# Two-layer transformer kernel on one Trainium2 core: TensorE's order of jobs, scores, weighted sums and transposes written out anew for both layers, and v read where it lies

## What is computed

```
x = x + attn_a(layernorm(x))      # scores over all 1024 keys
x = x + ffn(layernorm(x))
x = x + attn_b(layernorm(x))      # keys after the query masked
x = x + ffn(layernorm(x))

attn: qkv = x @ Wqkv + b; scores = q.k / sqrt(8); softmax; times v; @ Wout + bout
ffn:  (silu(x @ wg.T) * (x @ wu.T)) @ wd.T     # HIDDEN = 384
```

## Time and profile before

| | |
|---|---|
| median of 3 runs | 1573.65 us (1570.76 to 1574.26) |
| the profiled execution | 1573.21 us; span from first to last instruction 1571.4 us |
| TensorE (PE) busy | 92% of the span |
| VectorE (DVE) busy | 79% |
| ScalarE (ACT) busy | 62% |
| GpSimd (POOL) busy | 7% |
| granted clock of TensorE, mean | 0.965 of full |

### The profile page before, as it was taken

How to read it: one execution, slowest core, us unless ns; L and a number is a source line. 1 busy time by engine, 2 the same in 40 slices (tenths; PEclk the granted TensorE clock), 3 DMA queues, 4 the chain that set the end, 5 groups by cost and what they waited for, 6 DMA issues and landing times.

```text
span 1571.4 us, 26128 instructions
## 1 busy us (share of the span) xinstructions
PE 1438.6 (92%) x9625; PEld 701.7 (45%) x9625; DVE 1235.9 (79%) x3106; ACT 980.0 (62%) x1259; POOL 108.9 (7%) x210
## 2 busy tenths in 40 slices
PE   3699999999999999999988988999999999999888
PEld 2444344434444443444436654444444444444455
DVE  7589999999999998999937757787787877777254
ACT  4427777777777777777774432666666666666622
POOL 6020000000000000000001112000000000000010
PEclk9859999999999999999999985999999999999999
DMA  3720111111101111110001323111121112210000
GB/s 95 221 57 7 27 28 29 29 29 28 28 6 25 28 28 29 28 28 2 2 1 54 83 79 76 35 29 29 29 53 32 29 29 47 38 29 2 8 21 27
DMA packets 40055, 58.39 MB, mean 37 GB/s; under 512 B 7796, under 2 KB 19448, under 8 KB 39928
## 3 DMA queue, kind: packets, MB, share of 16 engines
q1 hardware_dynamic: 39928, 56.72, 15.2%
HBM read 36.77 MB, written 18.87 MB: 35 GB/s over the span
## 4 chain that ended last, share of the span: by engine, by line
PE 70%; DVE 18%; ACT 5%; issue 4%; DMA 2%; SPq 1%; POOL 0%; DVEq 0%; ACTq 0%; POOLq 0%
PE psum L995 25%; PE psum L1045 23%; DVE maxima L785 11%; PE psum L1009 6%; PE psum L1142 5%; PE psum L938 4%; ACT probs L559 3%; DVE junk L782 3%; PE psum L1147 2%; PE psum L1017 1%; PE psum L948 1%; DVE xn L706 1%; PE psum L1062 1%; DMA k_parts<-parts 1%; DMA qop<-shift_rows 1%
## 5 line engine op out<-in xcount | busy, mean ns | idle before, releaser
L559 ACT ACTIVATE probs<-psum 128x1024 f32<-128x1024 f32 (+3 forms) x896 | 794.2, 932 | 300.4 <-PE psum L1009 192.7
L785 DVE TENSOR_REDUCE maxima<-psum 128x1 f32<-128x512 f32 x1280 | 815.2, 684 | 72.8 <-PE psum L995 67.8
L995 PE MATMUL psum<-kop,qop 62*128 62x512 f32 (+3 forms) x1792 | 657.0, 465 | 56.5 <-DVE maxima L782 20.0
L1009 PE MATMUL psum<-qop,kop 64*128 64x512 f32 (+3 forms) x1792 | 498.2, 411 | 10.4 <-ACT probs L559 7.8
L995 PEld LDWEIGHTS psum<-kop,qop 62*128 62x128 f32 x1792 | 289.6, 191 | 487.6 <-DVE maxima L785 325.4
L1045 PE MATMUL psum<-probs,vwin 128*32 128x512 f32 (+3 forms) x3584 | 441.6, 565 | 3.9 <-ACT probs L559 2.0
L782 DVE CUSTOM_DVE_ANT_0 junk<-psum,mask 128x384 bf16<-128x384 f32 (+3 forms) x512 | 237.4, 487 | 75.3 <-PE psum L995 69.8
L1009 PEld LDWEIGHTS psum<-qop,kop 64*128 64x128 f32 x1792 | 242.0, 189 | 55.7 <-ACT probs L559 44.7
L1045 PEld LDWEIGHTS psum<-probs,vwin 128*32 128x32 f32 x3584 | 71.8, 109 | 105.5 <-issue 84.6
L1017 PE MATMUL psum<-half_ident,key_mask 64*128 64x64 bf16 x1024 | 92.7, 198 | 0.0
L1142 PE MATMUL psum<-ffn_xt,wffn 128*128 128x512 f32 x192 | 87.6, 594 | 0.0
(11 more groups left out here) (88 smaller groups left out, 709.9 us busy)
## 6 DMA issues: line engine op xcount, KB each, us to landing
qop<-q_parts SPq DMA_DIRECT2D x256, 64.0 KB
q_parts<-parts SPq DMA_DIRECT2D x32, 256.0 KB, 3.0
k_parts<-parts SPq DMA_DIRECT2D x32, 256.0 KB, 3.4
kop<-k_parts SPq DMA_DIRECT2D x64, 128.0 KB
kop<-k_parts SPq DMA_DIRECT2D x128, 64.0 KB
x<-in_L_attn_a_x SPq DMA_DIRECT2D x8, 256.0 KB, 4.4
qop<-shift_rows SPq DMA_DIRECT2D x128, 8.0 KB
out_x<-x SPq DMA_DIRECT2D x8, 256.0 KB, 2.3
```

The costliest lines, as they stand in the source:

```text
L559: nc.scalar.activation(probs[:, slot, :, c0:], psum[:, bank:bank + 2, c0:], ACT.Exp, scale=SCORE_SCALE).then_inc(probs_ready, 1)
L785: nc.vector.tensor_reduce(dst, src, AX_X, ALU.max).then_inc(ring_free, 1)
L995: mm(psum[:, slot, 0:width], qop[rows, buf, f, r, qb * P:(qb + 1) * P].bitcast(F32R), kop[rows, buf, r, kh * CHUNK:kh * CHUNK + width].bit ...
L1009: ins = mm(psum[:, bank + h, c0:], kop[rows, buf, pair, j * P:(j + 1) * P].bitcast(F32R), qop[rows, buf, f, pair, c0:].bitcast(F32R), star ...
```

## The change

The placement by weights is gone. Each layer's plan now has a string of letters for one turn: `j` a job, `s` a unit of scores, `p` the sums of a step, `H` and `h` the shift transposes (of the next window's half 0, of this window's half 1), `N` and `n` the transposes of the sums (this window's half 0, the last window's half 1). All engines walk the list that comes of it.

- Layer 0: the sums run two steps behind the scores (one before). 46 jobs stand ahead of the first scores.
- Layer 1: the sums stay one step behind. 44 jobs ahead. `alternate` takes the jobs so that neighbours are on different halves of the rows.
- The ring of three job banks, the two units of scores, the number of each operation and their shapes are as before.
- `vwin`, its POOL copies and the wait for them are gone: the sums load their weights from `v`.
- A window's operand load is issued by SP behind the shift of half 1 two windows earlier, no more behind the first sums.
- POOL's addition of a bias to all of x comes behind the first window's second shift in both layers.
- DVE does the inversion of the denominators at the place of `N` or `n` in the order, and the scaling behind the next job, sums or shift. Before, the inversion came one step later in a turn.

```diff
-SLOT_WEIGHTS = (1, 1, 1, 0)
+PROB_STEPS = PROBS // 2
...
-        cut = len(stream) if cut is None else cut
-        jobs = [(0, x) for x in stream[cut:]] + [(1, x) for x in stream[:cut]]
-        self.turn_steps = [(0, s) for s in range(turn, n)] + [(1, s) for s in range(turn)]
...
+                tiles = [(c, kh) for r in range(PAIRS) for kh in range(2) for c in (2 * r, 2 * r + 1)] if alternate \
+                    else [(c, kh) for c in range(HG) for kh in range(2)]
...
+        ends = {"H": ("shift", 0, 1), "h": ("shift", 1, 0), "N": ("norm", 0, 0), "n": ("norm", -1, 1)}
+
+        self.walk = []
+        jobs = taken = 0
+        last_unit = {}
+        for turn in range(-1, WINDOWS + 1):
+            j, u, k = jobs_ahead, 0, -sums_behind
+            for letter in order:
+                if letter == "j":
+                    w, x = turn + j // len(stream), stream[j % len(stream)]
+                    j += 1
+                    if 0 <= w < WINDOWS:
+                        self.walk.append(("job", w, jobs, x))
+                        jobs += 1
+                elif letter == "s":
+                    w, x = turn, units[u]
+                    u += 1
+                    if 0 <= w < WINDOWS:
+                        self.walk.append(("scores", w, taken, x))
+                        last_unit[w, x[0]] = taken
+                        taken += 1
+                elif letter == "p":
+                    w, x = turn + k // n, k % n
+                    k += 1
+                    if 0 <= w < WINDOWS:
+                        self.walk.append(("sums", w, last_unit[w, x], x))
+                else:
+                    kind, dw, f = ends[letter]
+                    if 0 <= turn + dw < WINDOWS:
+                        self.walk.append((kind, turn + dw, taken, f))
+                        taken += 1
+        self.jobs_all, self.units_all = jobs, taken
...
-PLANS = [Plan(causal=False, turn=3, cut=32 + 22, idle_steps=0, lead=7, project_at=(6, 8, 11)), Plan(causal=True, turn=2, cut=None, idle_steps=1, lead=12, project_at=(2, 4, 8))]
...
+PAIR_UNITS, HEAD_UNITS = ((0, 1), (2, 3)), ((0,), (1,), (2,), (3,))
+PLANS = [Plan(causal=False, heads=PAIR_UNITS, unit_ring=2, job_ring=3, alternate=False,
+              order="jssjjpjsjjpsjjjnssjjpjsjjpsjjjssjjpjsjjpsjHjjssjjpjsjjpsjjjssjjpjsjjpsjjjNssjjpjsjjpsjjjssjjpjsjjpsjjjhssjjpjsjjpsjj",
+              jobs_ahead=46, sums_behind=2, project_at=(9, 11, 14)),
+         Plan(causal=True, heads=PAIR_UNITS, unit_ring=2, job_ring=3, alternate=True,
+              order="sjjsjpjsjsjpjjjHsjjsjpjsjjspjjsjsjsjjnjjspjsjsjjpjsjjsjpjjsjsjpjjsjNjjsphjjspjjjspjjspjs",
+              jobs_ahead=44, sums_behind=1, project_at=(4, 6, 10))]
...
-        vwin = sb("vwin", [P, BUFS, VW + VPAD], F32)
...
+                for kind, w, number, f in plan.walk:
...
+                        shift_to_operand(f, w % BUFS, unit_base + number)
+                        if f == 1 and w + 2 < WINDOWS:
+
+                            wait(sp, sums_done, sums_base + w * plan.n)
+                            load_operands(w + 2, (w + 2) % BUFS)
...
-                def copy_v(w, buf):
-                    nc.gpsimd.tensor_copy(vwin[:, buf, :], v[:, bass.ds(w * VW, VW + VPAD)]).then_inc(vwin_ready, 1)
...
+                    if kind in ("job", "sums", "shift"):
+                        for f, jobs in unnegated:
+                            negate_max(f, job_base + jobs)
+                        for window, f in unscaled:
+                            scale_sums(window, f)
+                        unscaled, unnegated = [], []
+                    if kind == "job" and plan.ends_half(what):
+                        unnegated.append((what[0], number + 1))
+                    if kind == "norm":
+                        invert_denominators(w, what, unit_base + number)
+                        unscaled.append((w, what))
+                    if kind == "scores" and w == WINDOWS - 1 and what[1] == plan.heads[-1]:
...
-                    if s == 0:
-                        pe.wait_ge(vwin_ready, layer * WINDOWS + w + 1)
-                        slot = (buf * 2 * plan.n + 2 * s + c // 2) % PROBS
-                        at = (j * HG + c) * VH
-                        ins = mm(psum[32 * c:32 * c + 32, 7, c0:], vwin[:, buf, at:at + 32], probs[:, slot, c % 2, c0:],
+                        slot = (2 * (w * plan.n + s) + c // 2) % PROBS
+                        at = w * VW + (j * HG + c) * VH
+                        ins = mm(psum[32 * c:32 * c + 32, 7, c0:], v[:, at:at + 32], probs[:, slot, c % 2, c0:],
```

More of the change, by code:

```diff
@@ L118, in __init__ @@
-        units = [("exp", s, pair) for s in range(turn) for pair in range(2)]
-        events, due, start = [], {}, None
-        for k, x in enumerate(stream[:cut]):
-            events.append(("job", x))
-            if self.ends_half(x):
-                due[k + 4] = ("shift", x[0])
-                start = k + 4 + lead if x[0] == 0 else start
-            if k in due:
-                events.append(due.pop(k))
-            elif start is not None and k >= start and (k - start) % 3 == 0 and units:
-                events.append(units.pop(0))
@@ L283, in wait @@
             eng.wait_ge(s, value)
-        def windows(eng, body, turns):
-            for w in range(turns):
-                body(w, w % BUFS, w // BUFS)
         def pipeline(eng, body, first=0):
@@ L365, in _ @@
                 load_operands(1, 1)
-                unit = unit_base = layer * PLANS[0].units_all
+                unit_base = layer * PLANS[0].units_all
+                sums_base = layer * WINDOWS * PLANS[0].n
                 def shift_to_operand(f, buf, unit):
```

343 lines of the change are left out of this document (88 added, 255 removed).

## The result

The changed kernel takes **1502.96 us** (median, 1502.77 to 1506.32) against 1573.95 us of the kernel before on the same chip: ratio 0.9553, 95% interval 0.9527 to 0.9578. The forecast was 1540, in a range from 1500 to 1578. The direction and the range held; the gain of 71 us is more than twice the 33 us of the forecast.

A forecast was written before the change was run, and what follows sets the result against it. TensorE is busiest, but layer 0's step was read as set by DVE idling 0.31 us per group of sums; layer 1 is uneven, with DVE waits. 1573.2 + 22 (layer 0) - 59 (layer 1) + 4 (ends) = 1540 us, range 1500 to 1578.

The forecast's parts named there:

- The term of -59 us: Layer 1's turn, priced stretch by stretch between groups of sums: 27.8 us against 31.73, -3.9 a turn over 15 turns.
- jobs now go where ACT holds PE anyway: Layer 1: first of two reasons given for the shorter turn, -3.9 us; not sized by itself.
- the wait for denominators: Layer 1: DVE's 1.93 us wait a turn goes, since X stands two units behind its sums; second reason for -3.9 us.
- Layer 0, the long stretch: Layer 0, sums to sums with scores ahead of the first job: 3.52 us, DVE idle 0.54 in place of 0.31.
- Layer 0, the short stretch: Layer 0, from sums at 3.52 to sums at 5.64, with a job, scores and two jobs between, stepped in a line.
- The transposes: Layer 0, now mid-stretch where PE waits for DVE: 1.0 us a turn against 1.5, 0.33 each X, 0.17 each T.
- Ends: Both layers, work outside the full turns: layer 0 -4.8 and +7.5, layer 1 -2.4 and +3.9, together +4 us.
- The copies to `vwin`: POOL's 32 copies, removed: priced at nothing, since that work lies beside PE's; at most 1.32 us a turn.
- Every transpose in a new place pays: Rival, both layers: each moved transpose pays its change of array form, nothing hidden under DVE's waits; 1560 us, chance 15%.
- Slower: Rival, layer 0: the job behind scores starts later than stepped, DVE idles more; slower from 5.9 us per two steps; 12%.
- Layer 0 loses nothing, layer 1 reaches DVE's floor: Rival: no loss in layer 0, -84 us in layer 1, +4 for the ends, total 1493 us; chance 20%.
- three job banks force 0.31 us of idle DVE per group of sums: Layer 0 before the change: the least DVE idle time three banks allow, with a job right ahead of and behind sums.

## Why the prediction came out as it did

- **Layer 1, right, in the main for the reason given.** The term of -59 us measured -58.6, and all eleven stretches lie within 0.3 us of their price. What the prediction left open, the runs show: jobs alone give -0.86 us (1542.10), scores and transposes alone +0.66 (1574.59), both together 31.67 to 28.68 = -2.99, and alternating halves 0.86 more. Units and jobs have to move together: neither is worth much alone. Of the two causes that the prediction named, these runs speak for "jobs now go where ACT holds PE anyway"; the wait for denominators was over-weighted, since with it gone and 0.2 us of another, the turn gained 0.72 (1546.11). And some of the agreement is luck: the prices of the stretches have no term for alternating halves, without which the turn is 28.68, 0.9 above the forecast.
- **Layer 0, the long stretch, right in length** (3.52 stepped, 3.53 measured). DVE's idle time in it was not: 0.54 was said, and plain stretches have 0.34 counted the same way. The first new reduce comes 368.69 - 366.93 = 1.76 us behind the sums, as stepped, but DVE is busy with the ones before until 1.42 and not 1.22, because the sums come sooner. That follows from the next point.
- **Layer 0, the short stretch, the step that failed.** "Sums at 3.52, job 4.52, scores 4.85, jobs 5.09 and 5.32, sums at 5.64." Behind the sums at 381.68 the trace has the job at 0.99, a scores matmul at 1.00, the second scores and the next job at 1.33, and sums at 1.89. The halves of the array ran independently, where I had put scores and jobs in one line. So 2.12 us were priced where 1.90 were measured. 0.22 us too much for each of eight pairs is 1.8 us a turn, 26 us. The row to see it was there: in the earlier trace rows the job at 407.46 and the scores at 407.47 start together. It was used for the pitch of one half and not for this.
- **The transposes**, put at 1.0 a turn, cost 0.7: each X 0.34 (0.33 said), T nothing (0.17 said). That is 0.3 a turn, 5 us. The long stretches, at 0.01 more than stepped, take 1 us back, which makes the 30.
- **Ends**, the other mis-sized term: +4 said, -0.4 measured. In layer 0 three things make it up. Behind the last negation of half 0, +7.5 was said, and the way to the last scores is 2.5 us longer (45.14 to 47.66). Ahead, -4.8 was said, and it was -2.2: 0.3 up to the first negation, and 1.9 in the first turn, which was 46.67 against the usual 44.67 and is now 44.20 against 44.13. And one turn of the kernel before was 0.8 longer than the others, because PE waited for a shift's DMA once:

```profile
620.74 0.50 PE L1009 MATMUL psum<-qop,kop 64*128 64x512 f32 x2 [0.83 <-DMA qop<-shift_rows]
```

- **Outside of both attentions**, nothing was said and 3.5 us were gained, 1.55 of them ahead of the first job. The code there is unchanged, and the cause is open.
- **The copies to `vwin`** at nothing: right, 1.0001.
- **Rivals.** "Every transpose in a new place pays" (1560) fell in layer 0: put back behind the sums they cost 0.57 us a turn more. In layer 1 n alone, moved to its new place, gained 0.72 (1546.11). "Slower" needed two steps above 5.87; they took 5.43. "Layer 0 loses nothing, layer 1 reaches DVE's floor" (1493) was half right: layer 0 lost nothing, layer 1 stayed 1.7 us a turn above 26.1. Its number is the nearest, 10 us below the measured one, but in part by luck: the turns gave 66.7 us where it had 84, and the ends and what lies outside of them came out 8 us lower than said. A case between it and the forecast, layer 1 as forecast and layer 0 unchanged, 1573.2 - 59 = 1514, was not listed; it is 11 us above, 8 of them layer 0's own gain.
- That three job banks force 0.31 us of idle DVE per group of sums was right as a figure for the plain steps, 5.40 and 5.43 for two. That it bounds them alone was not: with a job ahead of the first scores, the unit banks held the stretch at 3.52. With other banks and scores ahead of the sums 2.60 a step was reached.

Open: why both bounds of the long stretch give the same 3.5 us, and whether an order for layer 0 exists that keeps 2.60 a step and hides the transposes.

## What to carry to other kernels

When work is packed on parts of the array, step each part as an engine of its own: a matmul waits for what is ahead of it on its own half. Price an order stretch by stretch, each by the engine that ends last in it, and move work of the other engines into the stretches that one engine holds; units and jobs must move together, since one alone gave about a quarter of the gain and the other a loss. An idle gap on a busy engine is worth only what the next bound leaves of it: the wait of 1.92 us for the denominators, gone with 0.21 of another, was worth 0.72, and in layer 0 a job moved up to DVE's gap behind the sums gained nothing, since another gap opened behind the third unit.

## What was unexpected of the hardware

- Matmuls on the two halves of the rows do not keep the order of the program among each other. In the raw records of the changed kernel, behind the sums at 376.06, a unit's second scores matmul starts at 377.065 with the job at 377.058, and its first, whose half the job holds, at 377.397; the next job, on the other half, starts at 377.400. The Trainium skill, page "TensorEngine Tiling (Array Packing)", Key Properties, says that tiles operate independently; this trace agrees. The Trainium skill, page "TensorE: Matmul & The Clock Gate", section "Step-by-step: what each phase is for", says that the matmuls themselves stay in program order; here the two starts 0.33 us apart are in the reverse of it, and the measurement decides. So the sentence ahead of the prediction by which TensorE keeps the program's order holds in these records within a half of the rows and not between the halves. ACT's exponential of that unit begins at 377.84, 0.44 behind the later of the two starts, although the matmul that the program puts last began first.
- A wait of 1.88 us a turn in front of one transpose went with a mean granted clock of 0.80 from 1040 to 1450 us, where the order with one job more ahead has 1.00. By the two levels, 0.5 and 1.0, that is 1.2 GHz for about 40% of the time, an estimate from that mean. The kernel took 1694.87 us, 7.6% more than with that order (1574.59; mean clock of the runs 0.891 and 0.965). Whether this one gap brings the clock down, or what comes with it, was not tried apart.
